# Softmax denominators from two f16 halves instead of one f32 matmul, with the spare bank's schedule shifted

## The reference

```python
q, k, v = [shape(layernorm(x) @ w) for w in (wq, wk, wv)]       # (2, 16, 2048, 64)
scores = einsum('bhqd,bhkd->bhqk', q, k) + position_bias        # relative position, 32 buckets
attn = softmax(scores, axis=-1)                                 # exp(s - max) / sum over keys of exp(s - max)
out = einsum('bhqk,bhkd->bhqd', attn, v) @ wo
x = x + layernorm(out)
```

## Time and profile before

| | |
|---|---|
| median of 3 runs | 2987.09 us (2985.86 to 2987.63) |
| the profiled execution | 2989.44 us, span 2987.6 us |
| TensorE matmuls busy | 2841.9 us, 95% of the span |
| GpSimd busy | 2275.2 us, 76% |
| VectorE busy | 1834.2 us, 61% |
| ScalarE busy | 1672.1 us, 56% |
| attention groups | from about 105 us to about 2764 us |

### The profile page before, as it was taken

The page is one execution under the profiler, slowest core; times in us unless marked ns, Lnnn a source line. Parts: engine busy times, 40 slices in busy tenths (PEclk is TensorE's granted clock), DMA queues, the critical chain, the costliest instruction groups (busy, mean ns, idle before and its releaser), DMA issues.

```text
span 2987.6 us, 49730 instructions
## 1 busy us (share of the span) xinstructions
PE 2841.9 (95%) x18785; PEld 1050.1 (35%) x18785; DVE 1834.2 (61%) x4663; ACT 1672.1 (56%) x2182; POOL 2275.2 (76%) x1033
## 2 busy tenths in 40 slices
PE   5799999999999999999999999999999999988997
PEld 2233333333333333333333333333333333322443
DVE  6566556565656656665656665665655566685666
ACT  3555565556555565555555555555555555556576
POOL 0588888888889888888888888888888888977000
PEclk8899999999999999999999999999999999999999
DMA  5000000000000000000000000000000000100001
GB/s 157 19 1 1 1 19 1 1 1 1 19 2 1 1 19 1 1 1 2 19 1 1 1 19 1 1 1 19 1 2 1 1 8 1 58 1 29 1 1 57
DMA packets 45137, 35.73 MB, mean 12 GB/s; under 512 B 21554, under 2 KB 43314, under 8 KB 44898
## 3 DMA queue, kind: packets, MB, share of 16 engines
q1 hardware_dynamic: 44898, 32.56, 3.8%
HBM read 27.60 MB, written 10.55 MB: 13 GB/s over the span
## 4 chain that ended last, share of the span: by engine, by line
PE 50%; DVE 22%; issue 20%; ACT 4%; POOL 3%; DMA 0%; SPq 0%; DVEq 0%; ACTq 0%; POOLq 0%
PE po L630 17%; PE st L600 14%; PE pre L612 5%; DVE mpart L1313 4%; PE pm L568 4%; DVE st L1330 3%; DVE pre L1310 3%; POOL acc L541 3%; PE st L855 3%; DVE pre L1305 2%; PE pm L574 2%; PE pm L660 2%; ACT prob L945 1%; PE pm L639 1%; DVE mpart L1310 1%
## 5 line engine op out<-in xcount | busy, mean ns | idle before, releaser
L541 POOL TENSOR_TENSOR acc<-acc,prob 128x1024 f32<-128x1024 f32 x896 | 2115.8, 2361 | 389.6 <-ACT prob L945 310.0
L945 ACT ACTIVATE prob<-st 128x1024 f32<-128x1024 f32 x1024 | 1015.9, 1021 | 914.2 <-DVE st L1330 814.8
L630 PE MATMUL po<-prob,v 128*64 128x512 f32 x4096 | 994.9, 606 | 0.0
L600 PE MATMUL st<-qk 64*128 64x512 f16 x6144 | 835.9, 378 | 21.1 <-ACT prob L945 16.5
L1305 DVE CUSTOM_DVE_ANT_0 pre<-pre,ew 128x512 f32<-128x512 f32 x448 | 300.7, 713 | 561.2 <-issue 561.1
L1310 DVE CUSTOM_DVE_ANT_0 pre<-pre,tab 128x512 f32<-128x512 f32 x704 | 475.1, 715 | 144.0 <-issue 144.0
L600 PEld LDWEIGHTS st<-qk 64*128 64x128 f16 x6144 | 293.5, 95 | 349.6 <-ACT prob L945 59.5
L630 PEld LDWEIGHTS po<-prob,v 128*64 128x64 f32 x4096 | 249.0, 136 | 442.2 <-issue 367.4
L600 PE MATMUL st<-eq,ek 64*128 64x512 f16 x2048 | 390.3, 378 | 0.0
L612 PE MATMUL pre<-qk 64*128 64x512 f16 x1600 | 309.9, 384 | 34.4 <-ACT ew L975 14.7
L1313 DVE TENSOR_REDUCE mpart<-pre 128x2 f32<-128x1024 f32 x224 | 273.9, 1223 | 98.2 <-PE pre L612 96.4
(11 more groups left out here) (204 smaller groups left out, 2341.0 us busy)
## 6 DMA issues: line engine op xcount, KB each, us to landing
t_scratch<-w_scratch SPq DMA_DIRECT2D x2, 2688.0 KB
inv_r<-inv SPq DMA_DIRECT2D x260, 1.0 KB, 1.7
qk<-x SPq DMA_DIRECT2D x8, 512.0 KB, 5.5
out<-qk SPq DMA_DIRECT2D x8, 512.0 KB, 3.6
w<-w_pairs SPq DMA_DIRECT2D x8, 384.0 KB, 3.7
t2f<-t_scratch SPq DMA_DIRECT2D x8, 384.0 KB, 4.8
t<-t_scratch SPq DMA_DIRECT2D x8, 384.0 KB, 3.3
den_c<-den_s SPq DMA_DIRECT2D x130, 2.0 KB, 1.7
```

Source lines behind the costliest of these rows:

```text
L541: nc.gpsimd.tensor_tensor(acc[g % 2][:, :, :], a, prob[:, n % RING, :, :], ALU.add).then_inc(sum_p, 1)
L600: last = nc.tensor.matmul(st[:, 2 * (n % 2) + h, :], w[64 * h:64 * h + 64, :], t[64 * h:64 * h + 64, :], start=(r == 0), stop=(r == len(te ...
L630: last = nc.tensor.matmul(po[64 * h:64 * h + 64, :], v[:, g // CHUNKS, j, 64 * h:64 * h + 64], prob[:, n % RING, h, :], start=(s == 0), st ...
L945: nc.scalar.activation(prob[:, n % RING, :, :], st[:, 2 * (n % 2):2 * (n % 2) + 2, :], ACT.Exp).then_inc(exp_done, 1)
```

## The change

The denominators come from f16. ScalarE rounds the finished sums to f16 at step 0 of the next group (`high_sums`), GpSimd takes the rest, f32 sum minus f16 part, into a second f16 tile after its addition of step 2 (`low_sums`), and TensorE adds both over the partitions with four f16 matmuls of 128x64 by 128x512 in place of two f32 ones. The f16 tiles live in a part of `ew16` that is free during attention. GpSimd's first addition of a group waits for its own `low_sums` of the group before and no longer for the denominators. Nearly every job of the spare bank gets another step, as do the steps of the inverse (4 to 5), of the f16 split of the output (9 and 10 to 10 and 12) and of the transposes in the last pair. The last call, after the last group, keeps the f32 form.

```diff
-JOBS = {1: ("den", 0), 2: ("proj", 0), 4: ("proj", 1), 6: ("proj", 2), 8: ("inv", 0), 11: ("max", 0), 12: ("y", 0), 14: ("y", 1),
-        15: ("proj", 3)}
-INV_AT, REST_AT, HIGH_AT, LOW_AT = 4, 6, 9, 10
+JOBS = {0: ("proj", 0), 2: ("proj", 1), 3: ("den", 0), 5: ("proj", 2), 7: ("proj", 3), 9: ("inv", 0), 12: ("max", 0),
+        13: ("y", 0), 15: ("y", 1)}
+SUMS_AT, INV_AT, REST_AT, HIGH_AT, LOW_AT = 2, 5, 6, 10, 12
-TR_AT = [(6, 13), (6, 15), (7, 0), (7, 2), (7, 3), (7, 4), (7, 5), (7, 6)]
+TR_AT = [(6, 14), (7, 0), (7, 1), (7, 2), (7, 4), (7, 5), (7, 6), (7, 7)]
...
+        unit16 = sb("unit16", [128, 64], f16)
+        acc16 = ew16[:, 1, 0, :].rearrange("p (n h q) -> p n h q", n=2, h=2)
...
+            def low_sums(G, g):
+                pool.wait_ge(acc_hi, G + 1)
+                nc.gpsimd.tensor_tensor(acc16[:, 1, :, :], acc[(g + 1) % 2][:, :, :], acc16[:, 0, :, :], ALU.subtract).then_inc(acc_lo, 1)
...
                     if s == 1:
-                        pool.wait_ge(den_ready, G + 1)
+                        pool.wait_ge(acc_lo, G)
...
+                    if s == SUMS_AT:
+                        low_sums(G, g)
...
-            def denominators(G, g):
+            def denominators(G):
+                pe.wait_ge(acc_lo, G + 1)
+                for n in range(2):
+                    for h in range(2):
+                        last = nc.tensor.matmul(pm[64 * h:64 * h + 64, :], unit16[:, :], acc16[:, n, h, :], start=(n == 0), stop=(n == 1))
+                last.then_inc(den_ready, 1)
+            def last_denominators(G, g):
                 pe.wait_ge(sum_p, (G + 1) * SUMS)
...
+            def high_sums(G, g):
+                act.wait_ge(sum_p, (G + 1) * SUMS)
+                act.wait_ge(den_ready, G + 1)
+                nc.scalar.activation(acc16[:, 0, :, :], acc[(g + 1) % 2][:, :, :], ACT.Copy).then_inc(acc_hi, 1)
...
+                    if s == 0:
+                        high_sums(G, g)
                     if s == 0 and g == CHUNKS - 1 and not last:
                         split_weights(i + 1)
```

More of the change, by code:

```diff
@@ L329, in layer @@
         sum_p = sem("sum_p")
+        acc_hi = sem("acc_hi")
+        acc_lo = sem("acc_lo")
         den_ready = sem("den_ready")
@@ L520, in _ @@
             nc.gpsimd.memset(unit[:, :], 1.0 / INV_UNIT).then_inc(set_pool, 1)
+            nc.gpsimd.memset(unit16[:, :], 1.0 / INV_UNIT).then_inc(set_pool, 1)
             nc.gpsimd.memset(wo16[:, :, :], 0.0).then_inc(wo_lo, 1)
@@ L737, in _ @@
                 piece(1, 1, u)
-            pe.wait_ge(set_pool, 2)
+            pe.wait_ge(set_pool, 3)
             pe.wait_ge(set_v, 15)
@@ L784, in jobs @@
                         elif kind == "den":
-                            denominators(G, g)
+                            denominators(G)
                         elif kind == "inv":
@@ L810, in _ @@
             pe.wait_ge(y_add, G_ALL * YJ + 1)
-            denominators(G_ALL, 0)
+            last_denominators(G_ALL, 0)
             def back(b, t):
```

## The result

The changed kernel takes 3279.59 us, the median of 4 runs (3277.05 to 3284.19), against 2987.02 us for the kernel before beside it: a ratio of 1.098, with a 95% interval of 1.0967 to 1.0993. The forecast was 3223 us, in a range of 3065 to 3290. The direction and most of the steps are right; the sum is 57 us short, a fifth of the change, and most of this chapter is about where those are. The time lies only 10 us inside the upper end of the range and is nearer to rival C's 3300 us than to the forecast. The profiled execution took 3284.19 us, its span is 3282.4 us, 294.8 more than before.

A forecast was written before the change was run, and what follows sets the result against it. TensorE's queue was taken as the bound. In four groups, 21.45 us of new waits less 4.5 old and 1.7 saved gave +15.2, times 15.5 +236 us: 3223 us, range 3065 to 3290.

The forecast's parts named there:

- rival C: All forecast waits come, and TensorE's granted clock falls too: a 3% loss is 80 us, 3300 us; chance 0.13.
- The saving: Denominators: four f16 matmuls cost 0.43 us, not 0.87, side by side; -0.43 a group, -28 us over 64 groups.
- GpSimd: low_sums taken as 2.5 us, GpSimd needing 39.9 us a group, where it had 37.4; nothing added to the forecast.
- Rival D: GpSimd bounds all groups, at 40.8 us against 41.3 now: 2955 to 2990 us; chance 0.04 for no change.
- Point 1: Pair n = 2: high_sums delays the copy, subtraction and read, so the second piece is late; 4.25 us in four groups.
- y 0: At step 13 it waits for the bank until the maxima's row is copied: 1.1 us in chunks 1 and 2, sum 2.2.
- Point 2: Pair n = 4: step 5's late exponential holds back proj 1's copy; 0.45, 0.7 and 0.3 us, sum 1.45.
- Point 3: Pairs n = 6 and 8: projections at odd steps keep VectorE from the next piece; 0.7 to 1.4 us, sum 3.65.
- Points 4 to 7: Waits in four groups: n = 10 0.9 us, n = 12 4.2, y 0 2.2, the maxima's DMA 4.8.
- A: ScalarE and VectorE take the new order without delaying a piece: 2959 us, or about 2975; chance 0.09.
- B: Only the delays at n = 2 to 8 count, the maxima's row comes in time: +94, 3081 us; chance 0.18.

The follow-up runs named there:

- v6: v5 with GpSimd's part of the inverse at step 5, low_wo after step 11, one transpose of the last pair earlier: 2969.8 us, ratio 0.9937.
- e6: The kernel before plus one unused GpSimd pass shaped like low_sums in each group of the first seven pairs: 2995.38 us, ratio 1.0024.
- e1: The kernel before with only the new steps of the jobs, denominators still f32, no extra pass: 3252.9 us, ratio 1.0892.
- e5: The changed kernel with the denominators at step 4 in place of 3, the inverse's steps following: 3264.29 us, ratio 1.0923.
- e4: The changed kernel with projections 2 and 3 at even steps 4 and 6 in place of 5 and 7: 3229.33 us, ratio 1.0813.
- e3: The changed kernel with the maxima back at step 11, y at 12 and 14, output split at 9 and 10: 3152.39 us, ratio 1.0557.
- v5: v4 with GpSimd's part of the inverse back at step 6: 3001.4 us, ratio 1.0045.
- e8: The changed kernel with the edits of both e3 and e4: 3100.11 us, ratio 1.0379.
- v4: The kernel before with f16 split sums, nearly old job order, rounding before step 2's exponential, low_wo moved, inverse's rest at 4: 3018.56 us, ratio 1.0103.

## Why the prediction was right, and where it was short

**What bounds the kernel: right.** TensorE's queue and waits of fractions of a microsecond decided it. The changes of the intervals come out of waits of TensorE gained or lost, of the shorter denominators, and in single intervals of its clock.

**The saving: right.** In chunk 3, where den does not wait, its four matmuls begin at 1548.16 and the piece behind them at 1548.70, 0.54 us; the f32 form took 0.96 (1680.96 to 1681.92). That is the 0.43 us of the forecast to 0.01: the column halves of the f16 matmuls run side by side. In v6, where no wait hides it, most groups are 0.36 to 0.50 shorter. The remark in the prediction that the saving would be worth nothing, since the reads limit and not the matmul, does not hold there: v6 is 19 us faster than the kernel before, of the 28 that were forecast. These are the lines of the kernel after:

```profile
1548.16 0.60 PE L653 MATMUL pm<-ew,unit 128*64 128x512 f16 x4
1548.70 0.39 PE L625 MATMUL pre<-qk 64*128 64x512 f16 x2
```

**GpSimd: harmless in this order, priced too high.** `low_sums` is 2.13 us with f16 output, 2.08 from start to start, where the bounds were 1.2 to 2.5 and 2.5 was taken. In v6 GpSimd needs 39.25 us in a chunk 3 (1579.53 to 1618.78, start to start of its first addition) and not 39.9. Rival D is out: after's GpSimd is at 74%, and e6 costs 0.24%.

**Point 1, the pair n = 2: right.** Chunk 0 of the timeline after; the marks are those of the earlier trace rows, and the second piece is due 1.95 us after the first (rows of other instructions are left out at the dots):

```profile
1767.96 1.05 ACT L1007 ACTIVATE ew<-acc 128x1024 f16<-128x1024 f32 x1
...
1768.17 0.39 PE L625 MATMUL pre<-qk 64*128 64x512 f16 x2
...
1768.91 0.59 ACT L948 ACTIVATE qk<-pm 128x512 f16<-128x512 f32 x1
...
1769.53 0.69 DVE L1320 SCALAR_TENSOR_TENSOR qk<-pm,qk 128x512 f16<-128x512 f32 x1 [2.52 <-ACT qk L948]
...
1771.60 0.39 PE L625 MATMUL pre<-qk 64*128 64x512 f16 x2 [1.32 <-DVE mpart L1339]
...
1773.32 1.94 PE L643 MATMUL po<-prob,v 128*64 128x512 f32 x8
...
1774.34 1.02 ACT L967 ACTIVATE prob<-st 128x1024 f32<-128x1024 f32 x1 [3.85 <-DVE st L1359]
1775.26 0.59 ACT L948 ACTIVATE qk<-pm 128x512 f16<-128x512 f32 x1
1775.88 0.69 DVE L1320 SCALAR_TENSOR_TENSOR qk<-pm,qk 128x512 f16<-128x512 f32 x1 [1.58 <-ACT qk L948]
1776.62 0.14 PEld L653 LDWEIGHTS pm<-ew,unit 128*64 128x64 f16 x4 [2.25 <-DVE qk L1320]
1776.63 0.62 PE L653 MATMUL pm<-ew,unit 128*64 128x512 f16 x4 [1.37 <-DVE qk L1320]
1777.18 0.39 PE L625 MATMUL pre<-qk 64*128 64x512 f16 x2
```

high_sums, the copy of proj 0, the subtraction, then the maximum, as foretold: 3.43 us from piece to piece, 1.48 late (1.55 forecast). The other chunks, 1 to 3: 1.22 (1.35), 0.03 (0.3), 1.73 (1.05). Only chunk 3 is far off: e1, without `high_sums`, has 0.78 there already, and the pass adds 0.95.

**The step that was missing: the denominators wait for the bank.** The lines from 1773.32 on. proj 1 at step 2 runs before the values and is read by ScalarE (1775.26) and VectorE (1775.88) at the end of the pair, behind the exponential of step 5 (1774.34), which is held back by the late piece; den at step 3 is due right after the values and needs the same bank. Values that den follows without a wait last 1.77 us to its start (1730.81 to 1732.58 in chunk 3); here it takes 3.31. So den stands 1.5 us in chunk 0, 1.8 in chunk 1 and 0.5 in chunk 2, a little more than the idle time in the brackets: 3.8 us in four groups that stood in no step. e5 gives the same: intervals 4 and 5 lost 1.0 us each and got 0.6 and 0.85 back as lateness. The prediction asked whether den would wait for GpSimd and never whether it would wait for its neighbour, though it noted the same hazard for y 0.

**Point 2: too high.** The cause is the same: the wait of den gives the pair n = 4 the time that it lacked. The second piece there is 0 late in chunks 0 and 1 and 0.57 in chunk 3, not 0.45, 0.7 and 0.3. e5 takes the wait away and the lateness comes back, 0.62 and 0.85. The waits of points 1 to 7 are 2.65 us below the forecast and den's 3.8 above it, so it is partly luck that the sum of the four groups came as near as it did.

**Point 3, the odd steps: right.** The pairs n = 6 and n = 8 of chunk 1 after; each is a projection at the odd step before, its copy, its subtraction or two, and the maximum that TensorE waits for:

```profile
1829.99 0.39 PE L625 MATMUL pre<-qk 64*128 64x512 f16 x2
...
1830.10 0.60 ACT L948 ACTIVATE qk<-pm 128x512 f16<-128x512 f32 x1 [1.50 <-PE pm L581]
...
1830.73 0.69 DVE L1320 SCALAR_TENSOR_TENSOR qk<-pm,qk 128x512 f16<-128x512 f32 x1 [2.38 <-ACT qk L948]
...
1831.34 1.22 DVE L1342 TENSOR_REDUCE mpart<-pre 128x2 f32<-128x1024 f32 x1
...
1832.61 0.39 PE L625 MATMUL pre<-qk 64*128 64x512 f16 x2 [0.50 <-DVE mpart L1342]
...
1836.20 0.39 PE L625 MATMUL pre<-qk 64*128 64x512 f16 x2
...
1839.41 0.39 PE L625 MATMUL pre<-qk 64*128 64x512 f16 x2 [1.09 <-DVE mpart L1342]
```

2.62 and 3.21 us from piece to piece, 0.67 and 1.26 late (0.7 and 1.4 forecast); chunk 0 has 0.67 and 0.86 (0.7 and 0.85). It was read off the job at step 15 in the earlier trace rows and held. e4 confirms it from the other side.

**Points 4 to 7: right in place, a seventh too high.** n = 10: 0.03 to 0.25 (0.15 to 0.3). n = 12: 0.69 to 0.95 in each chunk (1.05). y 0 waits 1.04 us in chunks 1 and 2 (1.1). The maxima's DMA holds up the scores of the pair n = 14, whose second piece is late by 0.83 to 1.29 (1.1 to 1.3). For the four intervals 2 to 5 the new waits are then 4.46 + 0.57 + 3.46 + 0.63 + 3.32 + 2.08 + 4.27 = 18.8 us (21.45 forecast) and 3.8 for den; less the 4.5 of before and 1.7 saved that makes +16.4, and the intervals have 181.94 - 165.14 = +16.8, against +15.2 forecast. e3 puts these points apart: its intervals 2 to 5 are 174.8 us, 7.1 less; points 5 to 7 measure 9.7, less the 2.2 that n = 12 had before, 7.5.

**The 57 us.** In profiled spans, 294.8 against the forecast's 236:
- The four regular intervals are 1.6 us worse than forecast, 15.5 times: 25 us. That is den's wait of 3.8 less the 2.65 that the other points were too high, and 0.4 that the marks don't give.
- Interval 1 has `low_wo`, 1.36 us of VectorE between the subtraction and a piece. After the change that place is late, so it counts:

```profile
1632.22 1.36 DVE L1381 SCALAR_TENSOR_TENSOR wo<-wo_s,wo 128x256 f16<-128x256 f32 x1
...
1634.96 0.39 PE L625 MATMUL pre<-qk 64*128 64x512 f16 x2 [2.33 <-DVE mpart L1339]
```

  Before, intervals 1 and 5 are equal (42.54 and 42.54). In e3 they are 48.43 and 47.12: 1.3 us a pair, 10 us in all.
- TensorE's clock, rival C in small. Interval 1 comes in two lengths, 50.9 us in the first two pairs of heads and 52.6 in the others. Here is the same place of the second and the third pair (range, length, PE, PEld, VectorE, ScalarE, GpSimd, granted clock, DMA share, GB/s) and the scores in each:

```profile
565.50:569.50 4.00, 4.00 (x30) 1.47 (x28) 1.40 (x5) 2.54 (x3) 2.20 (x2) 1.00 0.00 0
934.00:938.00 4.00, 4.00 (x22) 1.36 (x20) 0.59 (x2) 2.05 (x2) 1.01 (x1) 0.57 0.00 0
```

```profile
564.79 0.82 PE L613 MATMUL st<-qk 64*128 64x512 f16 x6 [1.11 <-DMA eq<-mrow]
565.45 0.38 PE L613 MATMUL st<-eq,ek 64*128 64x512 f16 x2
...
931.44 0.83 PE L682 MATMUL pm<-wo,o 128*128 128x256 f16 x6 [0.96 <-ACT mrow L955]
...
933.75 1.06 PE L613 MATMUL st<-qk 64*128 64x512 f16 x6 [1.16 <-DMA eq<-mrow]
934.59 0.64 PE L613 MATMUL st<-eq,ek 64*128 64x512 f16 x2
```

  With a granted clock of 0.57, which is mostly the lower level of 1.2 GHz, a pair of matmuls takes 0.64 us in place of 0.38, and the interval is 1.7 us longer. The granted clock in stretches of 4 us shows 16 such falls between 150 and 2800 us: seven in interval 1, seven in interval 6, and one each in the intervals 5 and 2 that stand out above. One of them, in the first interval 1, cost nothing, since that interval has 50.90 us all the same. The others cost 1.3 to 1.8 us each: about 24 us by what the intervals leave over. The mean clock fell from 0.985 to 0.978. Rival C had the clock right and its size wrong: it is lost in single stretches of 4 us, not through all groups.
- The start and the tail grew by 2.7 and 2.6 us: 5 us. The last pair of heads grew by 22.6, where 1.5 times 16.8, 1.3 and its one fall of the clock (1.7) would be 28.2: -6.

Together 25 + 10 + 24 + 5 - 6 = 58, of 59. The clock's share and the last pair's are read as what is left over, so that this adds up is no proof of them; den's wait is shown by e5, and `low_wo`'s share by v6, where interval 1 fell from v5's 43.5 to the 42.1 of interval 5 once `low_wo` stood in front of no piece of VectorE's.

**The rivals.** A (the cover holds) is refuted by every interval of chunks 0 and 1. B (points 1 to 3 alone, and the row in time) is refuted by the DMA wait at each of 63 hand-overs, and by e3, which is close to what B would have been: 3152, 71 us above B's own 3081. C holds for about 24 us. D is refuted above. That GpSimd's or ScalarE's extra pass is the main cause is refuted by e1.

## What to carry to other kernels

On engines that take their lists strictly in order, the fraction of a microsecond between an instruction's end and the moment its reader is asked for is the thing to tabulate before jobs are moved: for each place, who reads it, what stands ahead of that reader, and which resource the next user shares, the neighbour job included. Jobs in front of the values have the values' 1.8 us to be read in; jobs behind them are read on the next piece's time. The saving was real here, 19 us of the 28 that were forecast, and it came out only when the order that fed the bottleneck was left nearly alone.

## What the runs showed of the hardware

- The granted clock was 0.57 in a stretch of 4 us in the middle of dense work, after TensorE had stood for 0.96 and then 1.16 us. The same two waits at the same place leave it at 1.00 in another pair of heads (0.96 and 1.11). Between 500 and 2500 us no stretch of 4 us is below 0.9 in the kernel before or in v6. Waits of this size are not enough: e1, which has both, shows the longer interval 1 once in eight pairs. Nor are these two needed: e8, which has neither, falls to 0.59 (1535 to 1539 us) behind a piece that stood 2.33 us for `low_wo`. What tips it stays open.
- GpSimd's subtraction of 1024 columns took 2.13 us with an f16 output and one f16 input, and 2.36 us as an addition in f32; from start to start it is 2.08 against 2.47 (v6). That is 10% or 16% less, not half.
- A short operation can cost a queue far more than its length. In v4 0.2 us of GpSimd's work at step 4 cost 2.3 us of its queue in each group on average; with it at step 6 (v5) the kernel is 17 us faster.
